# Cross-attention and mixture of experts on one core: another order of work at the hand-over, record loads on GpSimd's queue, and a first product one slot ahead from slot 14 on

## The reference

```python
x = x + xattn(layernorm(x), ctx, ctx, Wq, bq, Wk, bk, Wv, bv, Wo, bo, alpha)   # 16 heads of 16
x = x + ffn(layernorm(x), Wr, W1, b1, W2, b2)

# ffn: 8 experts, each token goes to its best 2
logits = x @ Wr; probs = softmax(logits); w, idx = top_k(probs, 2); w = w / sum(w)
h = gelu(x @ W1[e] + b1[e])          # 256 -> 1024
y = h @ W2[e] + b2[e]                # 1024 -> 256
out = sum over the 2 experts of w * y
```

## Time and profile before

| | |
|---|---|
| median of 3 runs | 968.32 us (965.58 to 971.52) |
| profiled execution | 970.74 us |
| its span, first to last instruction | 968.9 us |
| mean granted TensorE clock | 0.977 |
| PE busy | 898.1 us (93%) |
| DVE busy | 697.2 us (72%) |
| ACT busy | 634.5 us (65%) |
| POOL busy | 415.5 us (43%) |
| share of the chain that ended last | PE 74%, issue 7%, DVE 6%, ACT 6%, POOL 3% |

### The profile page before, as it was taken

One profiled execution on the slowest core, in us unless ns is written; L12 is line 12 of the kernel. 1 busy time (PEld: TensorE's weight loads), 2 busy tenths in 40 slices (PEclk: granted clock), 3 DMA queues, 4 the chain that ended last, 5 costly groups with the idle time before them and its releaser, 6 DMA issues.

```text
span 968.9 us, 30634 instructions
## 1 busy us (share of the span) xinstructions
PE 898.1 (93%) x10701; PEld 789.8 (82%) x10701; DVE 697.2 (72%) x1833; ACT 634.5 (65%) x1236; POOL 415.5 (43%) x540
## 2 busy tenths in 40 slices
PE   3999999998999999989899699899999999999994
PEld 2788887787877877878777589799999999999993
DVE  7677888777987887779768577766666666666662
ACT  3688887787877877878857356455555455554551
POOL 6344456538546565385253532623222232222322
PEclk9799999999999999999979799999999999999998
DMA  5222122314132333253044773443333233332222
GB/s 150 70 72 89 41 83 80 112 41 128 57 99 76 126 123 103 92 171 111 20 139 134 275 273 52 85 93 52 51 52 51 47 52 52 52 51 48 46 30 22
DMA packets 61892, 84.82 MB, mean 88 GB/s; under 512 B 9872, under 2 KB 55312, under 8 KB 59568
## 3 DMA queue, kind: packets, MB, share of 16 engines
q1 hardware_dynamic: 47504, 64.26, 21.0%
q0 software_dynamic: 13296, 18.00, 11.1%
q10 hardware_dynamic: 944, 0.60, 0.2%
HBM read 49.86 MB, written 31.92 MB: 84 GB/s over the span
## 4 chain that ended last, share of the span: by engine, by line
PE 74%; issue 7%; DVE 6%; ACT 6%; POOL 3%; another core or an unknown queue 1%; DMA 1%; DVEq 0%; POOLq 0%; ACTq 0%
PE s_ps L711 10%; PE u_ps L711 10%; PE pv_ps L729 9%; PE gen L729 9%; PE gen L502 5%; PE gen L495 5%; PE s_ps L485 5%; PE u_ps L473 3%; PE pv_ps L519 2%; PE gen L544 2%; ACT pt L827 2%; PE gen L415 2%; PE gen L680 2%; PE gen L418 2%; PE gen L422 1%
## 5 line engine op out<-in xcount | busy, mean ns | idle before, releaser
L1567 POOL DMA_INDIRECT out<-yw,rb x71 | 110.3, 1553 | 269.4 <-DVE yw L1392 253.4
L928 ACT ACTIVATE h<-s_ps,b1t,inv 128x128 f32<-128x128 f32 x288 | 107.8, 457 | 89.6 <-PE s_ps L711 79.3
L928 ACT ACTIVATE h<-u_ps,b1t,inv 128x128 f32<-128x128 f32 x280 | 104.7, 459 | 87.4 <-PE u_ps L711 86.4
L1375 DVE TENSOR_SCALAR hs<-h,hsc 128x512 f16<-128x512 f32 x142 | 69.7, 491 | 120.4 <-ACT h L928 102.0
L827 ACT ACTIVATE pt<-gen,escale 128x512 f32<-128x512 f32 x128 | 86.8, 686 | 50.4 <-PE gen L502 34.5
L1377 DVE SCALAR_TENSOR_TENSOR hs<-h,hsc,hs 128x512 f16<-128x512 f32 x142 | 106.7, 751 | 5.1
L711 PE MATMUL s_ps<-xt,w1s 128*128 128x128 f16 x1728 | 104.8, 220 | 2.2 <-issue 2.2
L1517 POOL DMA_INDIRECT xrec<-rec,idx x64 | 77.8, 1215 | 60.9 <-DVE idx L1229 44.7
L711 PE MATMUL u_ps<-xt,w1s 128*128 128x128 f16 x1680 | 102.5, 220 | 0.9 <-issue 0.9
L711 PEld LDWEIGHTS s_ps<-xt,w1s 128*128 x1728 | 99.8, 99 | 2.8 <-issue 2.3
L729 PE MATMUL pv_ps<-w2s_sb,hs 128*128 x864 | 100.5, 272 | 0.5 <-issue 0.5
(11 more groups left out here) (251 smaller groups left out, 1741.8 us busy)
## 6 DMA issues: line engine op xcount, KB each, us to landing
wl<-L_ffn_W SPq DMA_DIRECT2D x16, 1024.0 KB
rb<-xrec SPq DMA_DIRECT2D x71, 132.5 KB
...
```

The source lines that it names most:

```text
L928: ins = act.activation(h32[n % HBANKS][:, m % HB, :], hbank[n % HBANKS][:, o:o + SLOT], ACT.Gelu, scale=inv1[:, bass.ds(ex, 1)].bitcast(F3 ...
L1567: pool.indirect_dma_start(out[:, :], bass.IndirectOffsetOnAxis(ap=rb[j][:, D + NE:D + NE + 1], axis=0), yw[s % 2][:, :], None, compute_op= ...
```

## The change

- **Hand-over.** VectorE copies the first turned records out before anything else of the second phase, and makes only the one scale that Gelu needs (`inv1`) before the next copy. `weight_low` of the last pair moves into slot 0, `residual(0)` behind the other scales, `heads_back(1)` behind the first split, `residual(1)` into slot 1.
- **TensorE.** The first slot's weight addresses are computed before T(0), the next ones between matmuls of the first products. T(0), T(1), T(2) and F(0), F(1) are spread between the last pair's steps. `project_out(1)` is in slot 0, `turn_y(0)` in slot 1, `logits(0)` in slot 2, `turn_y(1)` in slot 3, `logits(1)` in slot 4, `ranks` in slot 7.
- **From slot 14 on** F runs one slot ahead of S, not two: there is no F in round 12, then T(s+3), F(s+1), S(s).
- **ScalarE.** One activation loads Gelu's table before the slots. `record_high(0)` comes after Gelu of slot 2, `record_high(1)` after Gelu of slot 5 (before: 1 and 2), `route_exp` after Gelu of slot 7 (before 5).
- **VectorE.** `choose` follows `weigh(5)`, `counts` `weigh(6)`, `shares`, `positions` and `last_tables` `weigh(8)`, `weigh(9)`, `weigh(10)` (before: 1, 2, 5, 6, 7).
- **DMA.** `b2` is loaded before the records. The records of slots 0 to 9 are loaded by SP, those of slots 10 to 19 by GpSimd between two adds (before all by SP). Five experts' W2 are loaded before the last part of W2 is stored, three after it. The last pair's scatters follow the adds 9 to 12 (before 5 to 8).

```diff
@@ sync_program
+            for b in range(2):
+                sp.wait_ge(*at(f"v{b}", NP))
+            sp.dma_start(b2s[:, :, :], b2.partition_broadcast(P)).then_inc(sig("ldb2"), 16)
             sp.wait_ge(*at("soon", 1))
             sp.wait_ge(*dma("scat", 4 * (SOON_PAIR + 1)))
-            for b in range(2):
-                sp.wait_ge(*at(f"v{b}", NP))
-            for s in range(U - 1):
+            for s in range(U):
                 load_records(s)
-            store_w2(NP - 1)
             sp.wait_ge(*at("pv3", NP))
-            for e in range(NE - 1):
+            for e in range(W2_SOON):
                 load_w2(e)
...
@@ tensor_program
-            def first_product(s, ex):
+            def first_product(s, ex, ahead=()):
...
+                        for address in itertools.islice(ahead, 2 * DC):
+                            pe.to_reg(address)
...
+            experts = [expert_of(pe, 0)]
+            for address in first_addresses(experts[0]):
+                pe.to_reg(address)
+            turn_records(0)
             project_out(0, NP - 1)
+            experts.append(expert_of(pe, 1))
+            turn_records(1)
+            first_product(0, experts[0], first_addresses(experts[1]))
             heads_back(1, NP - 1)
-            for s in range(3):
-                turn_records(s)
-            experts = [expert_of(pe, s) for s in range(3)]
-            first_product(0, experts[0])
+            turn_records(2)
+            experts.append(expert_of(pe, 2))
+            first_product(1, experts[1], first_addresses(experts[2]))
             turn_on(1, NP - 1)
-            first_product(1, experts[1])
-            project_out(1, NP - 1)
-            turn_y(0, NP - 1)
             for s in range(NSLOT):
                 if s + 3 < NSLOT:
                     turn_records(s + 3)
-                if s + 2 < NSLOT:
-                    first_product(s + 2, experts[2])
+                if s + 2 < SHORT:
+                    first_product(s + 2, experts[2], second_addresses(experts[0]) if s == 0 else ())
+                elif SHORT - 2 < s < NSLOT - 1:
+                    first_product(s + 1, experts[1], second_addresses(experts[0]))
                 if s == 0:
+                    project_out(1, NP - 1)
+                if s == 1:
+                    turn_y(0, NP - 1)
+                if s == 2:
                     logits(0, NP - 1)
+                if s == 3:
                     turn_y(1, NP - 1)
-                if s == 1:
+                if s == 4:
                     logits(1, NP - 1)
-                if s == 4:
+                if s == 7:
                     ranks(NP - 1)
...
@@ scalar_program
             for s in range(NSLOT):
                 gelu(s)
-                if s == 0:
+                if s == 1:
                     o_turned(1, NP - 1)
-                if s == 1:
+                if s == 2:
                     store_x1(0, NP - 1)
                     record_high(0, NP - 1)
-                if s == 2:
+                if s == 5:
+                    store_x1(1, NP - 1)
                     record_high(1, NP - 1)
-                    store_x1(1, NP - 1)
-                if s == 5:
+                if s == 7:
                     route_exp(NP - 1)
@@ vector_program
+            take_records(0)
+            dve.tensor_scalar(inv1[:, :], k1[:, :], 25.0, float(ONE), ALU.subtract, ALU.mult).then_inc(sig("inv1"), 1)
+            take_records(1)
+            hidden_scales()
+            experts = [expert_of(dve, s) for s in range(2)]
             residual(0, NP - 1)
-            heads_back(1, NP - 1)
-            take_records(0)
-            take_records(1)
-            experts = [expert_of(dve, s) for s in range(2)]
             split_hidden(0, experts[0])
             take_records(2)
-            residual(1, NP - 1)
+            heads_back(1, NP - 1)
             split_hidden(1, experts[1])
...
@@ gpsimd_program
+            def load_records(s):
+                j = s % U
+                if s >= U + 5:
+                    pool.wait_ge(*dma(f"ldsoon{s % 5}", 1))
+                row = pool.value_load(slot_row[0:1, s:s + 1], min_val=0, max_val=NE * REGION)
+                pool.dma_start(rb[j][:, :], xrec_d[bass.ds(row, SLOT), :]).then_inc(sig(f"ldsoon{s % 5}"), 16)
+
             def add(s):
...
                 if s:
                     pool.wait_ge(*dma(f"add{(s - 1) % U}", (s - 1) // U + 1))
+                    if s - 1 + U < SOON:
+                        load_records(s - 1 + U)
```

More of the change, by code:

```diff
@@ L144, in build @@
     cnt_i = alloc(ctx, "cnt_i", [P, NE], I32)
+    gelu_one = alloc(ctx, "gelu_one", [P, 1], F32)
     s_ps = bank("s_ps", [P, 2, 512], F32)
@@ L673, in turn_records @@
                 g = xt_bank[:, 0:2 * DC * SLOT // 2].bitcast(F16)
-                pe.wait_ge(*dma(f"ldrec{s % U}", s // U + 1))
+                if U <= s < SOON:
+                    pe.wait_ge(*dma(f"ldsoon{s % 5}", 1 if s < U + 5 else 2))
+                else:
+                    pe.wait_ge(*dma(f"ldrec{s % U}", s // U if s >= SOON else 1))
                 if s:
@@ L758, in tensor_program @@
                     experts.append(expert_of(pe, s + 3))
-                later = second_addresses(experts[1]) if s + 1 < NSLOT else ()
-                second_product(s, experts[0], itertools.chain(later, first_addresses(experts[3]) if s + 3 < NSLOT else ()))
+                if s + 3 < SHORT:
+                    ahead = itertools.chain(second_addresses(experts[1]), first_addresses(experts[3]))
+                elif s + 3 == SHORT:
+                    ahead = second_addresses(experts[1])
+                elif s + 2 < NSLOT:
+                    ahead = first_addresses(experts[2])
+                else:
+                    ahead = ()
+                second_product(s, experts[0], ahead)
                 experts.pop(0)
@@ L915, in scalar_program @@
                     factors(1, it)
+            act.activation(gelu_one[:, :], mhalf[:, :], ACT.Gelu)
             def gelu(s):
@@ L919, in gelu @@
                 if s == 0:
-                    act.wait_ge(*at("scales", 1))
+                    act.wait_ge(*at("inv1", 1))
                 for q in range(QS):
@@ L1393, in weigh, with hidden_scales @@
                                   None, ALU.mult).then_inc(sig("yw"), 1)
+            def hidden_scales():
+                exponent(b1ss[:, :], kb[:, :])
+                step(dve.tensor_scalar(mk[:, :], k1[:, :], 4.0, None, ALU.add))
+                step(dve.tensor_tensor(mk[:, :], mk[:, :], kb[:, :], ALU.max))
+                step(dve.tensor_scalar(mk[:, :], mk[:, :], 1.0, None, ALU.add))
+                step(dve.tensor_scalar(hsc[:, :], mk[:, :], -float(ONE), 268.0 * ONE, ALU.mult, ALU.add))
+                step(dve.tensor_tensor(inv2[:, :], mk[:, :], k2[:, :], ALU.add))
+                dve.tensor_scalar(inv2[:, :], inv2[:, :], 155.0, float(ONE), ALU.subtract, ALU.mult).then_inc(sig("scales"), 1)
+            take_records(0)
[3 more added lines that the diff above has]
+            experts = [expert_of(dve, s) for s in range(2)]
             residual(0, NP - 1)
-            heads_back(1, NP - 1)
-            take_records(0)
-            take_records(1)
-            experts = [expert_of(dve, s) for s in range(2)]
             split_hidden(0, experts[0])
             take_records(2)
-            residual(1, NP - 1)
+            heads_back(1, NP - 1)
             split_hidden(1, experts[1])
@@ L1406, in vector_program @@
                     take_records(s + 3)
-                if s == 0:
-                    logits(0, NP - 1)
                 if s + 2 < NSLOT:
                     experts.append(expert_of(dve, s + 2))
+                if s + 2 < SHORT:
                     split_hidden(s + 2, experts[2])
+                elif SHORT - 2 < s < NSLOT - 1:
+                    split_hidden(s + 1, experts[1])
+                if s == 0:
+                    weight_low(NP - 1)
                 if s == 1:
+                    residual(1, NP - 1)
+                if s == 2:
+                    logits(0, NP - 1)
+                if s == 4:
                     logits(1, NP - 1)
@@ L1575, in gpsimd_program @@
                 add(s)
-                if 5 <= s < 9:
+                if 9 <= s < 13:
                     for i in range(2):
-                        scatter(s - 5, i, NP - 1)
+                        scatter(s - 9, i, NP - 1)
             pool.wait_ge(*dma("scat", 4 * NP))
@@ L1586, in build @@
     HBANKS = 4
+    W2_SOON = 5
+    SHORT = 14
     with ExitStack() as f:
+        b2s = alloc(f, "b2s", [P, NE, D], F32)
         rb = [alloc(f, f"rb{i}", [P, REC], I32) for i in range(U)]
```

34 lines of the change are left out of this document (12 added, 22 removed).

## The result

| | us, median | lowest to highest | runs |
|---|---|---|---|
| kernel before | 967.91 | 965.58 to 971.52 | 4 |
| changed kernel | 989.15 | 986.28 to 991.14 | 4 |

The ratio is 1.0214, 95% interval 1.0173 to 1.0255: 21 us slower, where 978 was forecast with a range to 989. The profiled execution took 991.14 us with a span of 989.5, against 970.7 and 968.9 before, so 20.6 us of span have to be found.

A forecast was written before the change was run, and what follows sets the result against it. TensorE's work was taken as the steady-state bound, so only stretches with gaps could change: 12.5 + 1.5 - 2.8 - 1.8 = +9.4 on the profiled 970.7 gives 980.1, forecast as 978 us against 968.3, range 967 to 989.

The forecast's parts named there:

- Hand-over: Start of the second phase to S(0)'s end: an earlier first copy on VectorE gains 11.3 us, bounds 9 to 13.
- A wait of 1.0: Hand-over, before turn_on(1): TensorE waits 1.0 us for heads_back(1), on VectorE behind the split of slot 0.
- 9 (clock falls): Lower bound of the hand-over's gain: 9 us instead of 11.3 if the clock falls.
- Slot 1: Before S(1): new wait of 5.5 us for the bank that residual(1) frees, bounds 4 to 6.5, plus 1.5 for clock.
- The term for the clock: After the wait of slot 1: 1.5 us added because matmuls run at half clock after such a gap.
- Slot 3: Before T(7): new wait of 6.0 us for slot 0's add, behind the record after Gelu 5; bounds 5 to 7.5.
- Slot 7: Waits of 3.4 us before T(10) and 4.8 before ranks, plus 1.5 for the clock.
- GpSimd's loads: Adds 1 to 10 on GpSimd: each plain load costs 1.9 us, so adds come every 6.4.
- The rival that the queue is the bound: GpSimd's queue: if a load costs over 2.1 us, more weigh steps wait; 984 to 990 us, chance 0.15.
- Last tables and slots 14 to 70: Tables on VectorE lose 2.8 us in place of 5.6; from slot 14 the one-slot lead costs 0.
- S(70)'s own 0.5: Last slot: S(70) computes its addresses in place, 3.14 us against 2.62, +0.5.
- The end: After S(70): the last add starts at +3.7 to +4.2 in place of +6.5, -2.3 us; -1.8 with S(70)'s own 0.5.

The follow-up runs named there:

- a0_again: The changed kernel unchanged, run again on another chip: 975.19 us against 956.85 for the kernel before, ratio 1.0184.
- a6_heads: Changed kernel with heads_back(1) moved ahead of residual(0) and the split of slot 0 on VectorE: 969.95 us, ratio 1.0138 to the kernel before.
- a1_residual: Changed kernel with residual(1) on VectorE moved into slot 0, ahead of the split of slot 2: 970.17 us, ratio 1.0138 to the kernel before.
- c1_all_three: Changed kernel with early residual and record steps, slots 10 to 19's record loads on SP, and route_exp behind Gelu 8: 954.31 us, ratio 0.9978 to kernel before.
- a2_records: Changed kernel with residual(1) in slot 0, turn_y and logits steps in slots 0 to 3, records behind Gelu 1 and 3: 960.82 us, ratio 1.0051 to kernel before.
- a4_ranks: Changed kernel with ranks in slot 9 instead of 7, positions, last_tables and scatters one slot later: 975.17 us, ratio 1.0205 to the kernel before.
- a3_loads_sp: Changed kernel with the record loads of slots 10 to 19 issued by SP, none by GpSimd: 971.06 us, ratio 1.0155 to the kernel before.
- b1_tail: Kernel before with only the one-slot lead of F over S from slot 14 on: 953.73 us, ratio 0.9969 to the kernel before.

## Why the prediction was wrong

The direction was right, and the place and the releaser of each of the four waits in slots 1 to 7. The size was not: +20.6 of span against +9.4. By the ledger's lines:

- **Hand-over, -11.3 forecast, -6.1 measured (-7.4 in a0_again).** This is the step that failed. "A wait of 1.0" before turn_on was 4.09. I dated the split of slot 0 by what it needs (3.6 after F(0)) and not by what VectorE does before it: the scales, about 3 us, two number reads, 1.6, and the residual, 1.3, stand ahead of it, and heads_back behind it. TensorE reached the wait 1.3 earlier than I thought, VectorE 1.7 later, and after it F(2) ran at half clock (5.11 for 2.84). a6_heads takes this out and gives 5.2 us. The bound of "9 (clock falls)" covered the clock alone. The numbers of this wait are a0_again's; in the first profile S(0) ends another 1.3 later. That profile starts at half clock and has the gaps in F(1) and ScalarE's stop. How the 1.3 divides is not shown: beside a0_again they are all of it, beside a1_residual and c1_all_three, which start in the same way without gaps and end S(0) at 20.7 and 20.8, gaps and stop would cost 3.3.
- **Slot 1, +7.1 forecast, +9.3 (+8.3).** Wait 5.5 forecast and 6.02 measured, released by the residual as said. The term for the clock was mis-sized: S(1) took 5.28, 2.5 too long, not 1.5; 0.4 more were lost between S(1) and S(2). a1_residual shows the cause: with the residual moved, wait and half clock are gone.
- **Slot 3, +8.3 forecast, +7.8 (+7.3).** Right: 5.20 of wait for 6.0, the add behind record_low behind Gelu 5, yw waiting for the landing; 1.7 for the clock. a2_records, with the records early, takes the wait out.
- **Slot 7, +9.7 forecast, +10.6 (+10.5).** Right in sum: 2.35 for 3.4 and 4.85 for 4.8, and 2.2 for the clock instead of 1.5. a4_ranks and c1_all_three show the cause as the exponential behind choose.
- **GpSimd's loads.** 1.5 us each by a3_loads_sp, under my 1.9; adds 6.0 to 6.5 apart, where I said 6.4. The rival that the queue is the bound is wrong for this kernel, where other waits cover it, and right for a2_records, where they don't.
- **Last tables and slots 14 to 70, -2.3 forecast (with S(70)'s own 0.5), -1.4 (-1.8).** The lead of one slot costs nothing (b1_tail), and S(70)'s 0.5 measured 0, so the tables gave 1.4 and not 2.8.
- **The end, -2.3 forecast, -0.3 (-0.7).** The add chain gave 2.7, and a term of 2.5 was missing that the forecast put at nothing without a reason: the closing drain, 5.59 for 3.05. Neither the page nor a timeline shows it, the view of the program's last line does.

The misses are 5.2 at the hand-over, 2.2 in slot 1, 0.4 in slots 3 to 7, 0.9 and 2.0 behind them, and 0.8 ahead of the last values: 11.5, where the spans give 11.2. Nearly all have one sign, since I left out costs and no gains.
